# Adaptive-norm transformer pair on one core: the modulation moved to the end of the head, gates kept as columns, and unused products on TensorE

## What is computed

```python
mod = (_silu(L0_c) @ L0_wmod).reshape(4, 6, 1, -1)
sa, ca, ga, sb, cb, gb = (mod[:, i] for i in range(6))
ga = (2 * (ga >= 0) - 1) * jnp.maximum(jnp.abs(ga), 0.25)      # gb likewise
h = _layernorm(x) * (1 + ca) + sa
x = x + ga * _L0_attn_ref(h, ...)     # gated delta rule: 16 key heads, 32 value heads, T = 256
h = _layernorm(x) * (1 + cb) + sb
x = x + gb * _L0_ffn_ref(h, ...)      # quantised weights, 256 -> 704 -> 256
# layer 1: the same with L1_c, L1_wmod; softmax attention, then a sum of eight factors with a bias
```

## Time and profile before

| | us |
|---|---|
| median of 3 runs | 1414.9 |
| the 3 runs | 1408.9, 1415.26, 1414.9 |
| the profiled execution, whole | 1408.95 |
| its span, first to last instruction | 1407.2 |
| head, until the first merge product | 127.5 |
| loop, from there to the end of its block | about 1020.7 |
| the rest (feed-forward of layer 0, layer 1) | about 259 |

### The profile page before, as it was taken

One profiled execution on the slowest core, in us unless ns is written; L12 is line 12 of the kernel. 1 busy time (PEld: TensorE's weight loads), 2 busy tenths in 40 slices (PEclk: granted clock), 3 DMA queues, 4 the chain that ended last, 5 costly groups with the idle time before them and its releaser, 6 DMA issues. The chain is left out here.

```text
span 1407.2 us, 29942 instructions
## 1 busy us (share of the span) xinstructions
PE 1214.1 (86%) x10528; PEld 993.8 (71%) x10528; DVE 948.1 (67%) x2293; ACT 815.7 (58%) x2257; POOL 741.5 (53%) x1181
## 2 busy tenths in 40 slices
PE   8765999999999998999999998999987738978774
PEld 8565887888878787888888787888876624445453
DVE  4885787787878887787878877787823133134776
ACT  4433666766767666766767666766745323125871
POOL 1676858567675858567675857668573000020001
PEclk9885999999999999999999999999989677988997
DMA  4022230413122130413122130411102031000002
GB/s 160 30 77 40 65 95 10 103 24 82 34 72 50 57 96 10 103 24 82 34 71 48 60 101 6 102 25 43 35 16 59 1 101 51 0 0 1 1 2 94
DMA packets 139226, 72.81 MB, mean 52 GB/s; under 512 B 112525, under 2 KB 128421, under 8 KB 137157
## 3 DMA queue, kind: packets, MB, share of 16 engines
q1 hardware_dynamic: 139076, 70.89, 19.5%
HBM read 57.06 MB, written 13.78 MB: 50 GB/s over the span
## 5 line engine op out<-in xcount | busy, mean ns | idle before, releaser
L781 POOL TENSOR_TENSOR tmp<-Dm,Tn 64x31 f32<-64x31 f32 (+15 forms) x496 | 268.5, 541 | 97.1 <-DMA Dm<-blk_in_scratch 61.8
L784 POOL TENSOR_TENSOR Tn<-Tn,tmp 64x31 f32<-64x31 f32 (+15 forms) x496 | 280.1, 565 | 38.9
L619 DVE SCALAR_TENSOR_TENSOR cv<-bank,cw,cv 128x255 f32<-128x255 f32 (+2 forms) x384 | 155.0, 472 | 85.8 <-ACT cv L470 85.8
L757 POOL TENSOR_TENSOR ro<-ss,mhalf 128x4 f32<-128x4 f32 x64 | 64.5, 1008 | 238.6 <-ACT junk L532 207.7
L619 DVE SCALAR_TENSOR_TENSOR cqk<-bank,cw,cqk 128x255 f32<-128x255 f32 (+2 forms) x384 | 154.8, 471 | 8.3 <-ACT cqk L470 8.2
L398 PE MATMUL bank<-wo,OTs 128*128 128x256 f32 x512 | 138.9, 406 | 7.4 <-ACT OTs L562 7.4
L684 DVE SCALAR_TENSOR_TENSOR BP<-bank,cj,E 128x512 f32<-128x512 f32 (+1 forms) x256 | 142.8, 611 | 2.3
L532 ACT ACTIVATE junk<-og 128x129 f32<-128x129 f32 x256 | 79.8, 312 | 101.0 <-issue 87.1
L688 DVE TENSOR_TENSOR R<-Vs,bank 128x256 f32<-128x256 f32 x64 | 26.9, 421 | 137.6 <-PE bank L364 137.6
L398 PEld LDWEIGHTS bank<-wo,OTs 128*128 128x128 f32 x512 | 93.5, 198 | 22.7 <-ACT OTs L562 11.0
L540 ACT ACTIVATE ogn<-og,ro 128x128 f32<-128x128 f32 x256 | 81.9, 397 | 33.8 <-POOL ro L757 33.8
(11 more groups left out here) (214 smaller groups left out, 3513.1 us busy)
## 6 DMA issues: line engine op xcount, KB each, us to landing
rvz<-in_L_attn_W_qkvz SPq DMA_DIRECT2D x16, 512.0 KB, 5.4
x<-alpha_scratch SPq DMA_DIRECT2D x8, 1024.0 KB, 6.3
alb<-alpha_scratch SPq DMA_DIRECT2D x7, 1024.0 KB, 6.3
rqk<-in_L_attn_W_qkvz SPq DMA_DIRECT2D x16, 256.0 KB, 2.6
wo<-in_L_attn_W_out SPq DMA_DIRECT2D x16, 256.0 KB, 5.7
blk_in_scratch<-BP SPq DMA_DIRECT2D x256, 16.0 KB, 1.5
tinv_scratch<-Tn SPq DMA_DIRECT2D x32, 128.0 KB, 2.1
tinv_t_scratch<-Tt SPq DMA_DIRECT2D x32, 128.0 KB, 2.2
```

Source lines behind the costliest of these rows:

```text
L619: nc.vector.scalar_tensor_tensor(d, bk[:, t * T:(t + 1) * T - s], cw[p][:, first + t, TAPS - 1 - s:TAPS - s], d, ALU.mult, ALU.add).then_i ...
L781: pool_step_done(nc.gpsimd.tensor_tensor(t, Dm[:, j, j + 1:BLK].unsqueeze(2).broadcast_to([SLOTS, r, c]), Tn[:, j, 0:c].unsqueeze(1).broad ...
L784: pool_step_done(nc.gpsimd.tensor_tensor(Tn[:, j + 1:BLK, 0:c], Tn[:, j + 1:BLK, 0:c], t, ALU.subtract), kh * NTS + 2 * j + 4)
```

## The change

Eleven edits that belong together, all but the last two in the head:

1. four unused products of 128x256 with the unit matrix as PE's first work, and sixteen ahead of the loop's first step, after a wait for all modulation values (`modT` at 12);
2. the modulation parts that aren't needed at once leave the place ahead of `spread_alpha`; parts 2 to 5 of layer 0 and 0 to 5 of layer 1 are now made, all as columns, behind `lead_gram(3)` and between the `lead_qk` of g = 4 to 6 (8, 8, 12 and 12 products);
3. `gate_rows`, `place_gate_rows`, the POOL chain, and the DRAM round trip of the gates are gone; DVE makes the gates from columns in four operations of 128x32 after `dve_split_vz(1, 1)`;
4. ACT places the ten late parts (`place_mods`) after `act_silu_z(0, 0, 2)`;
5. `alpT` lies in Tt, PE turns alpha earlier (after `lead_gram(0)`), and ACT splits the v,z weights of head 0 earlier;
6. POOL clears U and UT at its very beginning;
7. SP waits for "zero" only ahead of `sp_blocks_read(0, 0)`, so that `sp_blocks_in(0, b)` waits for nothing but its BP;
8. POOL's `pool_inverse_start(0)` goes ahead of `pool_vpow(0, 0)`;
9. `lead_qk(1)` goes ahead of `spread_alpha(1)`, and ACT's `lead_tap0(1)` ahead of `place_alpha(1)`;
10. `residual` waits for `gates_act` in place of the DMA;
11. in the next block PE spreads the gates with 32 products of 128x128 (`spread_gates`; gates 0 and 1 ahead of the layer norm's turns, 2 and 3 behind them), and ACT copies them in eight operations of 128x512, two ahead of `ln_scalar` and six behind it.

```diff
-            mrow = [A2[0:B].rearrange("b s n -> b (s n)"), OTs[0:B].rearrange("b h c t -> b (h c t)")]
-            gabs = Tt[0:B].rearrange("b j i -> b (j i)")
-            gsign = UT[0:B].rearrange("p b u t -> p (b u t)")[:, 0:4 * D]
-            alpT = U[0:NVH].rearrange("p b u t -> p (b u t)")
+            alpT = Tt[0:NVH].rearrange("s j i -> s (j i)")
+            gcol = modT[:].rearrange("p l n b -> p (l n b)").rearrange("p (g r) -> p g r", g=4)[:, :, 2 * KC * B:3 * KC * B]
+            gabs = sb("gabs", [P, 4, KC * B], ctx=s1)
+            gpos = sb("gpos", [P, 4, KC * B], ctx=s1)
...
-                sp.wait_ge(sem("gates"), 2)
-                sp.dma_start(gates_dr.rearrange("g b d -> b g d"), gsign.rearrange("b (g d) -> b g d", g=4)).then_inc(sem("gates_out"), 16)
                 sp_load_alb(1)
                 sp_load_vz(1)
-                sp.wait_ge(sem("zero"), 2)
                 for b in range(B):
                     sp_blocks_in(0, b)
...
+                sp.wait_ge(sem("zero"), 2)
                 sp_blocks_read(0, 0)
...
                 pe.wait_ge(sem("const"), 3)
+                for _ in range(4):
+                    nc.tensor.matmul(bank[0][:, 0:T], ident, eye[:], start=True, stop=True)
...
-                def modulation(l, ms):
+                def modulation(l, ms, bk=bF):
...
-
-                def gate_rows(l):
-                    wait(pe, "mrow", l)
-                    for i, m in enumerate((2, 5)):
-                        for k in range(KC):
-                            last = nc.tensor.matmul(bank[4][0:B, i * D:(i + 1) * D], csil[:, l, k, :], wmod[:, l, k, m * D:(m + 1) * D],
-                                                    start=(k == 0), stop=(k == KC - 1))
-                    last.then_inc(sem("gate_mm"), 1)
...
                 def turn_alpha(h):
-                    pe.wait_ge(sem("alb_act"), 3 + h)
                     for t in range(4 * h, 4 * (h + 1)):
-                        last = nc.tensor.transpose(bank[5 + h][0:NVH, t % 4 * P:(t % 4 + 1) * P], gx[:, t, :], ident)
+                        last = nc.tensor.transpose(bank[4 - h][0:NVH, t % 4 * P:(t % 4 + 1) * P], gx[:, t, :], ident)
                     last.then_inc(sem("alpha_tr"), 1)
...
-                pe.wait_ge(sem("wmod_in1"), 48)
-                pe.wait_ge(sem("modT"), 2)
-                modulation(0, (3, 4))
-                modulation(1, (0, 1, 3, 4))
                 pe.wait_ge(sem("alpha"), 1)
                 pe.wait_ge(sem("ln_hT"), KC * B)
                 spread_alpha(0)
+                lead_qk(1)
                 spread_alpha(1)
-                lead_qk(1)
                 pe.wait_ge(sem("const1"), 1)
                 lead_gram(0)
-                gate_rows(0)
+                pe.wait_ge(sem("modT"), 2)
+                turn_alpha(0)
+                turn_alpha(1)
                 spread_alpha(2)
                 spread_alpha(3)
                 lead_qk(2)
                 lead_gram(1)
-                turn_alpha(0)
-                turn_alpha(1)
-                gate_rows(1)
                 lead_qk(3)
                 lead_gram(2)
                 lead_gram(3)
-                pe.wait_ge(sem("modT"), 8)
-                pe.wait_ge(sem("mrow"), 2)
+                pe.wait_ge(sem("wmod_in1"), 48)
+                pe.wait_ge(sem("alb_act"), B)
+                pe.wait_ge(sem("alpha_t"), 2)
+                modulation(0, (2, 3))
                 for g in range(B, LEAD_QK):
                     b = g - B
                     lead_qk(g)
+                    if b == 0:
+                        modulation(0, (4, 5))
                     if b:
                         lead_gram(g - 1)
+                    if 0 < b < 3:
+                        modulation(1, range(3 * b - 3, 3 * b))
                     if b < LEAD_VZ:
                         if b:
                             for c in range(NC):
@@ -1055,6 +1046,9 @@
                             pe_vt(0, 0, b - 1, 0)
                 for c in range(NC):
                     pe_z(0, 0, LEAD_VZ - 1, c)
+                pe.wait_ge(sem("modT"), 2 * MODS)
+                for _ in range(16):
+                    nc.tensor.matmul(bF[:, 0:T], ident, eye[:], start=True, stop=True)
                 steps(pe_step, 0, 0)
                 for kh in range(1, NKH):
                     steps(pe_step, kh, kh % 2)
...
-                def place_gate_rows(l):
-                    act.wait_ge(sem("gate_mm"), l + 1)
-                    nc.scalar.activation(mrow[l], bank[4][0:B, :], ACT.Copy).then_inc(sem("mrow"), 1)
+                def place_mods(n, l, ms):
+                    act.wait_ge(sem("mod_mm"), n)
+                    for m in ms:
+                        place_mod(l, m)
...
                 place_alpha(0)
                 lead_silu(0)
+                lead_tap0(1)
                 place_alpha(1)
-                lead_tap0(1)
-                act.wait_ge(sem("mod_mm"), 3)
-                for l, m in ((0, 3), (0, 4), (1, 0), (1, 1), (1, 3), (1, 4)):
-                    place_mod(l, m)
+                act_split_vz(0, 0)
+                for h in range(2):
+                    act.wait_ge(sem("alpha_tr"), h + 1)
+                    nc.scalar.activation(alpT[:, h * 512:(h + 1) * 512], bank[4 - h][0:NVH, :], ACT.Copy).then_inc(sem("alpha_t"), 1)
                 lead_silu(1)
                 place_alpha(2)
                 place_alpha(3)
                 lead_tap0(2)
-                place_gate_rows(0)
-                act_split_vz(0, 0)
+                act_split_qk(1, 1)
                 lead_silu(2)
-                for h in range(2):
-                    act.wait_ge(sem("alpha_tr"), h + 1)
-                    nc.scalar.activation(alpT[:, h * 512:(h + 1) * 512], bank[5 + h][0:NVH, :], ACT.Copy).then_inc(sem("alpha_t"), 1)
                 lead_tap0(3)
-                place_gate_rows(1)
-                act_split_qk(1, 1)
                 lead_silu(3)
...
                 act_silu_z(0, 0, LEAD_VZ - 1)
+                place_mods(5, 0, range(2, MODS))
+                place_mods(5, 1, range(MODS))
                 act_split_qk(2, 0)
...
                 dve_split_vz(1, 1)
+                ch = Chain(dve, "gate_chain")
+                dve.wait_ge(sem("modT"), 2 * MODS)
+                ch.after(nc.vector.scalar_tensor_tensor(gabs[:], gcol, -1.0, gcol, ALU.mult, ALU.max))
+                ch.after(nc.vector.tensor_scalar(gabs[:], gabs[:], 0.25, None, ALU.max))
+                ch.after(nc.vector.tensor_scalar(gpos[:], gcol, 0.0, 2.0, ALU.is_ge, ALU.mult))
+                nc.vector.scalar_tensor_tensor(gcol, gpos[:], -1.0, gabs[:], ALU.add, ALU.mult).then_inc(sem("gates"), 1)
                 dve_split_qk(2, 0)
...
                 nc.gpsimd.memset(tmp[:], 0.0).then_inc(sem("const1"), 1)
+                for t in (U, UT):
+                    nc.gpsimd.memset(t[:].rearrange("p b u t -> p (b u t)"), 0.0).then_inc(sem("zero"), 1)
...
                 pool.wait_ge(sem("wvz_high"), 1)
                 split_low("wvz", 0, rvz, wvz)
-                ch = Chain(pool, "gate_chain")
-                for l in range(2):
-                    cols = slice(l * 2 * D, (l + 1) * 2 * D)
-                    pool.wait_ge(sem("mrow"), l + 1)
-                    ch.after(nc.gpsimd.tensor_scalar(gsign[:, cols], mrow[l], 0.0, 2.0, ALU.is_ge, ALU.mult))
-                    ch.after(nc.gpsimd.tensor_scalar(gsign[:, cols], gsign[:, cols], -1.0, None, ALU.add))
-                    ch.after(nc.gpsimd.tensor_tensor(gabs[:, cols], gsign[:, cols], mrow[l], ALU.mult))
-                    ch.after(nc.gpsimd.tensor_scalar(gabs[:, cols], gabs[:, cols], 0.25, None, ALU.max))
-                    nc.gpsimd.tensor_tensor(gsign[:, cols], gsign[:, cols], gabs[:, cols], ALU.mult).then_inc(sem("gates"), 1)
                 pool.wait_ge(sem("wqk_high"), 2)
                 split_low("wqk", 1, rqk, wqk)
-                pool.wait_ge(sem("alpha_out"), 16)
-                nc.gpsimd.memset(U[:].rearrange("p b u t -> p (b u t)"), 0.0).then_inc(sem("zero"), 1)
-                pool.wait_ge(sem("gates_out"), 16)
-                nc.gpsimd.memset(UT[:].rearrange("p b u t -> p (b u t)"), 0.0).then_inc(sem("zero"), 1)
+                pool_inverse_start(0)
                 pool_vpow(0, 0)
-                pool_inverse_start(0)
                 pool_inverse(0, 0, BLK - 1)
...
-            if b == 0:
-                nc.vector.wait_ge(sem("gate_in0"), 16)
-                if (layer, m) != (0, 0):
-                    nc.vector.wait_ge(sem("gate_in1"), 48)
+            nc.vector.wait_ge(sem("gates_act"), 2 * (2 * layer + m) + b // 2 + 1)
...
-                for n in range(4):
-                    sp.dma_start(gates[:, n // 2, n % 2].rearrange("p b d -> p (b d)"),
-                                 gates_dr[n:n + 1].rearrange("g b d -> g (b d)").broadcast_to([P, B * D])).then_inc(sem(f"gate_in{min(n, 1)}"), 16)
...
             def _(act):
+                def place_gates(n):
+                    for h in range(2):
```

(23 more changed lines are left out.)

13 lines of the change are left out of this document (6 added, 7 removed).

## The result

| | before | after |
|---|---|---|
| median, 11 runs of each side by side, us | 1411.65 | 1402.01 |
| lowest and highest, us | 1406.0, 1419.24 | 1398.46, 1407.19 |
| profiled execution, whole, us | 1408.95 | 1398.46 |
| its span, us | 1407.2 | 1396.7 |

The forecast was 1403 (1394 to 1412), the likeliest outcome faster by over 0.5%.

What follows compares the result with a forecast made beforehand. The first inverse was taken to bound the head. Merge -8.6, head 0 -3.1 and next block +2.8 gave -8.9 us: 1400.1 from the profiled 1408.95, 1406.0 from the median 1414.9, middle 1403 (1394 to 1412).

Steps and rivals of the forecast that it cites:

- Modulation out of alpha's way: In the head, moving modulation products from ahead of the alpha spread starts that spread 6.3 us earlier.
- Blocks end 8.1 earlier, inverse 15.5 earlier: Head 0's blocks end at 60.8 us; its inverse starts at 67.2 and runs 39.1 us.
- Rival (d): In the head, the gate chain isn't what holds SP: about 0 gained, 1409 us; chance 0.06.
- Start products: Four unused products at the kernel's start: between +0.9 us and a gain of perhaps 2, taken as 0.
- The second chain: Lead work of g = 4 to 7 beside the inverse: `lead_qk(4)` 6.6 us earlier, modT complete at 104.8.
- Sixteen products on the path: Ahead of the loop's first step: they take 9.8 us, merge at 118.9 instead of 127.5, 8.6 earlier.
- Head 0 shorter by 3.1: In the loop, the clock raised by the sixteen products makes head 0 take 63.1 us instead of 66.2.
- Rival (a): Around the first merge, the clock doesn't rise or falls again; sixteen products cost 15.1 us: +3.6, 1412.6 us; chance 0.10.
- The next block: Behind the loop: -1.6 us at the gates' wait, weight turns and feed-forward start 2.8 us later, all told.
- The sum: Whole kernel: merge -8.6, head 0 -3.1, next block +2.8, together -8.9 us.
- middle of two bases: Whole time: 1400.1 us from the profiled execution, 1406.0 from the median 1414.9; the middle, 1403, was taken.
- The stretched scans: DVE scans beside busy POOL are blocked ones; the earlier inverse could lose 1 to 2 us in g = 4's scans.

Runs made afterwards that it cites:

- experiment 3: Changed kernel with all ten modulation parts of layers 0 and 1 back ahead of the alpha products: median 1405.0 us, ratio 0.9966 to the kernel before.
- experiment 1: The kernel before, with no edit, profiled in one more execution: whole time 1402.55 us.
- experiment 4: Changed kernel without the four unused start products: median 1399.4 us, ratio 0.9939 to the kernel before.
- Experiment 5: Changed kernel without the sixteen unused products ahead of the loop's first step, the wait for modT kept: median 1396.6 us, ratio 0.9903 to the kernel before.
- experiment 7: Kernel before with only sixteen unused products added between the first half of v and the first merge: ratio 0.9972 to the kernel before.
- experiment 6: Changed kernel with six more unused products inside the first merge, three ahead of each of its last two stages: median 1395.8 us, ratio 0.9895.
- experiment 9: Changed kernel, unused products moved (eight behind last z product, nine before first merge), six inside that merge, all gate spreads ahead of layer norm: 1389.0 us, 0.9849.

## Why the prediction was right, and where it wasn't

**Modulation out of alpha's way** (-6.3 for the spread). Right in kind: -5.6 in the profiled pair, and experiment 3, with 40 products there instead of 24, put 9.3 us back. But 10.23 us is the longest of the three courses seen of before; against its other two executions the spread starts 2.6 us sooner and 1.8 later. The term was taken from one execution as if it belonged to the program, and "half clock" was read from the price, where the granted clock of that trace reads 1.00 (experiment 1).

**Blocks end 8.1 earlier, inverse 15.5 earlier.** Blocks -7.6 (61.3 against 60.8 forecast), inverse -15.0 (67.67 against 67.2), 39.2 us long as forecast. Of this, 9.4 us are the distance between alpha and the inverse, which is 49.6 to 50.2 us before and 40.6 to 41.8 in the eleven executions with the edits: 2.0 from alpha to the end of the blocks (1.8 forecast) and 7.4 from there to the inverse (13.8 to 6.4). Rival (d) falls with it. The 7.4 belong to the gate chain, the clearing and the order on POOL together; these edits were not tried apart.

**Start products**, taken as 0: they delayed the first modulation by 0.9 (6.29 against 5.38), and alpha by no more than it varies by itself; experiment 4 finds no effect on the time.

**The second chain.** `lead_qk(4)` at 61.74 (61.4 forecast), the last silu 7.1 earlier (7.0), `modT` complete at 104.5 (104.8). Right to the tenths, and in part by luck: how much of the products stuck out (1.0) and what the clock gave (1.4) were estimates that no run measures apart, and the chain slipped by 4.4 us in experiment 4, and the inverse's return with it (3.9). That was not in the prediction.

**Sixteen products on the path.** 9.2 us from 104.5 to 113.7 (9.8), clock up at 109.0 after 4.5 us (4.5), merge at 118.2 (118.9), PE not waiting for U. That the clock term fits is luck of this execution: in the second one the clock was high from the start, they took 7.0 us (105.06 to 112.07), and the merge stood at 116.5. Experiment 5 confirms by removal that they are on the path, and that U, forecast at 112.0, is there at 112.5.

**Head 0 shorter by 3.1**: the step of the sum that failed. It shrank by 1.4 (66.2 to 64.8; 64.5 in the second execution), and experiments 5 and 7 give the products 0.4 to 0.8 and 0.3 to 0.5 of it. The cause was named rightly, the clock in the first step: with it high throughout, experiment 6 measured 63.04. What was wrong is that products ahead of the merge keep it up: it fell again at 122.7, inside the merge, behind the first wait between its stages, and stood at 0.50 for 6.7 us, where the prediction wanted 1.00. Rival (a) had this as its second half ("or falls again"), but tied it to sixteen products at 15.1 us, which didn't come. Without them head 0 still took 65.2 us, 0.8 to 1.0 less than before; why, is open.

**The next block.** Residual -2.5 instead of -1.6, since the first two spreads ran at full clock (3.81 us for sixteen products) where half was assumed. Spreads 2 and 3 took 5.5 us (4.8), and the first feed-forward product stands 29.85 us behind the residual against 25.2: +4.7, with the -2.5 a net of +2.2 up to there, and as the second feed-forward group took 2.62 us instead of 2.02, +2.8 from the loop's end to layer 1, as forecast. The forecast's own terms give 4.8 - 1.6 = 3.2 there, not 2.8 (and 5.9, not 5.7, at half clock), so that it met the 2.8 exactly is chance.

**The sum.** Merge -9.4 (-8.6; ACT's copy -9.7), head 0 -1.4 (-3.1), next block +2.8 (+2.8), and in layer 1 -2.0 that was not forecast: span -10.5 against -8.9. Of the last, about 1 us is steady (from the first feed-forward product to the end 229.2, 228.7, 228.8 us before and 227.8, 227.7 after); a low-clock stretch in the scores of layer 1, 1291 to 1298 in the first profile of before, is 6.8 to 6.9 us long in all three executions of before and 3.4 in both of after. Why it is, is open. So the total was met by errors of 1 to 2 us against each other, within a spread from run to run that is larger than any of them; that the sum comes so close is luck. The median came out at 1402 where the middle of two bases gave 1403: the medians differ by 9.6 us (8.9 forecast), and 1411.65, the median of before in eleven runs, happened to lie at that middle.

**The stretched scans.** After, DVE's two scans over half the columns take 0.71 us beside an idle POOL and 1.54 and 1.45 us at 80.75 and 94.35, beside the inverse; so scans beside a busy POOL are the longer ones. But the 1 to 2 us that the prediction feared there didn't come: the six rows of scans from 67 to 96 us take 8.95 us together, the like six before, from 74 to 103 us, 9.52, and ACT's last silu came at the time forecast. The longer scans agree with the rule weighed in the prediction, of the Trainium skill's page "SBUF — State Buffer", section on the two separate sides; whether the loser stands still for a whole instruction the rows can't tell.

**Left open**: whether ACT's turn of the inverse, put ahead of its last silus, makes the late courses of the head rarer; it wasn't tried. Nor was each of the three edits of experiment 9 timed enough to be separated by times. Why the loop takes up to 7 us more or less with no edit in it is open too.

## What to carry to other kernels

Look at two or three executions before pricing a stretch in which the clock changes: distances that stay the same across executions are the program's; a price may rest on them, on the others only with a spread beside it. Unused products paid here only where TensorE would wait anyway: inside the merge's waits they gave 1.9 us, ahead of it, on the path, they cost 4.0 to 5.6 and gave 0.4 to 0.8. Work that has no reader soon belongs in the engine's known waits, which holds for the modulation, moved out of alpha's way, and for the gates' products, moved into the layer norm's.
